# Latent attention with a gated feed-forward: the rope swaps' transfers on ScalarE's queue instead of SyncE's

## What is computed

```
xn = layernorm(x)
q = (xn @ wq) per head: 128 q_nope, 64 q_pe;   kva = xn @ wkv_a: 64 ckv, 64 k_pe
ckv = rmsnorm(ckv) * kv_norm_scale;            k_nope, v = ckv @ wkv_b per head
q_pe, k_pe = rope(q_pe), rope(k_pe)            # [x1*cos - x2*sin, x2*cos + x1*sin]
out = softmax(causal(q k^T / sqrt(192))) v @ wo
g = silu(((silu(xn gate_w^T * gate_s)) * (xn up_w^T * up_s)) down_w^T * down_s)
return x + out * g
```

## Time and profile before

| | |
|---|---|
| time, median of 3 runs (lowest to highest) | 1220.86 us (1214.34 to 1222.77) |
| the profiled execution: its time, its span | 1209.94 us, 1208.1 us |
| TensorE: matmul, weight load | 83%, 71% of the span |
| VectorE, ScalarE, GpSimd | 69%, 60%, 54% |
| granted TensorE clock, mean | 0.93 |

### The profile page before, as it was taken

How to read it: one execution, slowest core, us unless ns; L and a number is a source line. 1 busy time by engine, 2 the same in 40 slices (tenths; PEclk the granted TensorE clock), 3 DMA queues, 4 the chain that set the end, 5 groups by cost and what they waited for, 6 DMA issues and landing times.

```text
span 1208.1 us, 26429 instructions
## 1 busy us (share of the span) xinstructions
PE 1006.8 (83%) x10576; PEld 859.9 (71%) x10576; DVE 828.0 (69%) x1359; ACT 720.4 (60%) x1033; POOL 655.2 (54%) x448
## 2 busy tenths in 40 slices
PE   6665888888888888798888878888798987888998
PEld 5554767777777766677767767677677776777887
DVE  6755766876677777777787668777867687583234
ACT  1336666666667666666666566666766676673222
POOL 3837466745665466655674566465736664531232
PEclk7877998998899999999999899999999899898999
DMA  5038899998999989989999899999989899994001
GB/s 153 18 60 172 153 159 185 189 170 166 176 186 158 180 181 163 177 165 182 176 171 168 167 177 171 169 176 180 183 163 172 171 177 198 164 176 97 1 19 53
DMA packets 600042, 184.92 MB, mean 153 GB/s; under 512 B 574960, under 2 KB 586864, under 8 KB 599920
## 3 DMA queue, kind: packets, MB, share of 16 engines
q1 hardware_dynamic: 595440, 182.57, 81.0%
q10 hardware_dynamic: 4480, 0.66, 0.3%
HBM read 30.09 MB, written 2.10 MB: 27 GB/s over the span
## 4 chain that ended last, share of the span: by engine, by line
PE 29%; DMA 21%; DVE 16%; SPq 14%; POOL 14%; issue 3%; ACT 1%; ACTq 0%; POOLq 0%
DMA pT<-hl 16%; PE s_ps L637 9%; PE s_ps L535 7%; POOL hl L1097 6%; PE slot_ps L535 5%; DVE part_max L937 5%; SPq L478 5%; DMA sinT<-sinT_dram 4%; DVE hl L946 4%; SPq L465 4%; SPq L471 4%; POOL pe L1097 4%; PE o_ps L653 2%; POOL q_swap L1097 2%; PE o_ps L535 1%
## 5 line engine op out<-in xcount | busy, mean ns | idle before, releaser
L807 ACT ACTIVATE prob<-s_ps,neg_max 128x1024 f32<-128x1024 f32 (+7 forms) x384 | 327.6, 864 | 288.8 <-DVE neg_max L940 139.8
L1097 POOL TENSOR_TENSOR hl<-prob,hl 128x1024 f16<-128x1024 f32 x128 | 274.9, 2148 | 262.5 <-ACT hl L743 255.5
L937 DVE TENSOR_REDUCE part_max<-s_ps 128x1 f32<-128x1024 f32 (+7 forms) x256 | 245.2, 987 | 213.7 <-PE s_ps L637 202.8
L653 PE MATMUL o_ps<-v,pT 128*128 128x65 f16 x2176 | 238.2, 197 | 153.6 <-DMA pT<-hl 150.1
L653 PEld LDWEIGHTS o_ps<-v,pT 128*128 128x128 f16 x2176 | 206.9, 98 | 169.3 <-DMA pT<-hl 165.1
L743 ACT ACTIVATE hl<-prob 128x1024 f16<-128x1024 f32 (+7 forms) x384 | 294.9, 804 | 0.0
L946 DVE TENSOR_TENSOR hl<-prob,hl 128x1024 f16<-128x1024 f32 (+7 forms) x256 | 248.9, 1011 | 0.4 <-ACT hl L743 0.4
L654 PE MATMUL o_ps<-v,pT 128*128 128x64 f16 x2176 | 238.2, 198 | 0.0
L655 PE MATMUL o_ps<-v,pT 128*128 128x65 f16 x2176 | 237.1, 195 | 0.0
L655 PEld LDWEIGHTS o_ps<-v,pT 128*128 128x128 f16 x2176 | 209.0, 102 | 0.0
L654 PEld LDWEIGHTS o_ps<-v,pT 128*128 128x128 f16 x2176 | 208.0, 99 | 0.0
(11 more groups left out here) (196 smaller groups left out, 2007.9 us busy)
## 6 DMA issues: line engine op xcount, KB each, us to landing
cosT<-cosT_dram SPq DMA_DIRECT2D x32, 256.0 KB, 3.5
sinT<-sinT_dram SPq DMA_DIRECT2D x32, 256.0 KB, 3.9
q_swap<-q_pe SPq DMA_DIRECT2D x128, 64.0 KB, 2.0
pT<-hl SPq DMA_TRANSPOSE x256, 4.9
wq_sb<-in_L_attn_wq_dram SPq DMA_DIRECT2D x8, 384.0 KB, 4.5
acc<-in_L_attn_x_dram SPq DMA_DIRECT2D x4, 512.0 KB, 6.5
wo_sb<-in_L_attn_wo_dram SPq DMA_DIRECT2D x8, 256.0 KB, 3.3
x_in<-in_L_attn_x_dram SPq DMA_DIRECT2D x1, 2048.0 KB, 8.3
```

Source lines behind the costliest of these rows:

```text
L653: nc.tensor.matmul(whole, pT[:, b, :], v[:, kb, 0:LORA + 1], start=(m != 1 and b == 0), stop=False)
L807: nc.scalar.activation(prob_of(u, m), score_bank(u, m), ACT.Exp, bias=neg_max[:, r:r + 1]).then_inc(exp_done, 1)
L937: nc.vector.tensor_reduce(part_max[:, u % 2, m:m + 1], src, AX.X, ALU.max).then_inc(part_done, 1)
L1097: return lambda: nc.gpsimd.tensor_tensor(dst, a, b, op)
```

## The change

The function `swap` moves from SyncE's program to ScalarE's. ScalarE calls it directly behind the copy into `q_pe`, with the same two waits and the same four transfers; SyncE no longer has them.

```diff
@@ SyncE
-            def swap(g, pair):
-                half = ROPE // 2
-                sp.wait_ge(act_freed, after("act", (f"pe{g}", pair)))
-                n = group_no(g, pair)
-                if n >= 1:
-                    before = GROUP_ORDER[(n - 1) % NG], (n - 1) // NG
-                    sp.wait_ge(pool_done, POOL.after((f"rope{before[0]}.2", before[1])))
-                for i in range(4):
-                    a, b = slice(i * half, (i + 1) * half), slice((i ^ 1) * half, (i ^ 1) * half + half)
-                    sp.dma_start(q_swap[a, :], q_pe[b, :]).then_inc(swapped, 16)
...
-            swap(3, 0)
-            swap(0, 0)
             for u in range(NU):
                 pair, k = divmod(u, PU)
                 turn_first(u)
-                for name in jobs_at(u - 1):
-                    if name[0].startswith("pe"):
-                        swap(int(name[0][2:]), name[1])
                 turn_rest(u)
@@ ScalarE
+            def swap(name, pair):
+                half = ROPE // 2
+                n = group_no(int(name[2:]), pair)
+                act.wait_ge(act_freed, after("act", (name, pair)))
+                if n >= 1:
+                    before = GROUP_ORDER[(n - 1) % NG], (n - 1) // NG
+                    act.wait_ge(pool_done, POOL.after((f"rope{before[0]}.2", before[1])))
+                for i in range(4):
+                    a, b = slice(i * half, (i + 1) * half), slice((i ^ 1) * half, (i ^ 1) * half + half)
+                    act.dma_start(q_swap[a, :], q_pe[b, :]).then_inc(swapped, 16)
...
                     copy(q_pe[:], ps).then_inc(act_freed, 1)
+                    swap(name, pair)
```

## The result

| | before | after |
|---|---|---|
| time, median (lowest to highest) | 1220.86 us, 3 runs (1214.34 to 1222.77) | 1238.66 us, 4 runs (1233.41 to 1249.2) |
| profiled execution: time, span | 1209.94, 1208.1 us | 1239.47, 1237.6 us |
| granted TensorE clock | 0.933 | 0.933 |

The changed kernel is slower: ratio 1.0166, 95% interval 1.0089 to 1.0243, some 18 us. The forecast was 1227, and of its cases "within 1%" had the best chance (0.38). What came is "slower by over 1%" (0.34): above the forecast's own range (1216 to 1237) and inside the wide one (1197 to 1264), which reached that far only because it covers the rivals. The time lies between the forecast (+6) and rival B (+29).

A forecast was written before the change was run, and what follows sets the result against it. It took SyncE's queue, with swaps at 1.5 us each, to be on the path. Per pair -1.2 (unit 6), -1.2 (unit 9), +3.0 (unit 14 with unit 12's gain) made +0.6; together +6 us, 1227, own range 1216 to 1237.

The forecast's parts named there:

- within 1%: Whole kernel: time less than about 12 us from before, no difference that can be told; chance 0.38.
- slower by over 1%: Whole kernel: slower by more than about 12 us, through rivals B and C and a little of the forecast's spread; chance 0.34.
- rival B: ScalarE bounds ten units a pair; delays eat units 6 and 9's gain, unit 14 costs 3.8 us: 1250 us, chance 0.20.
- Units 6, 9 and 12: Second transposes and tables go out earlier once SyncE is rid of the swap: gains 1.2, 1.2 and 0.8 us.
- the late exponentials are covered by SyncE: Units 6 and 9: next unit's exponentials move from 387.43 to 388.8 and 412.76 to 413.4, hidden by SyncE's lateness.
- its cut of unit 6 from 1.9 to 1.2: Unit 6: transpose 1.9 us earlier, but POOL's low half of unit 8 can gain only 0.7; 1.2 taken.
- The hold: ScalarE at each swap: held 2.6 us, four issues at the median 0.584 us each plus some 0.15 for the copy.
- rival C: Swap issues on ScalarE wait for transposes being issued half the time, 32 x 1.4 = 45 us more: 1272 us, chance 0.13.
- Unit 14: ScalarE stands still for rope.2 until 454.2, then issues until 456.7; unit 15's exponentials come late, cost 3.0 us a pair.
- See nothing behind it to take it up: Behind unit 14: nothing later absorbs the 3.0 us delay, so it counts in full.
- +2 for the start: First pair's own swaps: two in the set-up at 0.5 us, those in units 0 and 1 +1.5 us.
- Rival A: SyncE's queue is all that counts; ScalarE's delays vanish under its waits, unit 14 costs 1.1 us: 1207 us, chance 0.27.

The follow-up runs named there:

- e4: Against the changed kernel: no swap transfers and no waits for them, q_swap set to zero once; 1183.14 us, 0.9685 of before.
- e1: Against the changed kernel: only unit 14's swap goes back to SyncE, the others stay on ScalarE; 1219.5 us, 1.0012 of before.
- e5: Against the changed kernel: rope.1 writes into the sine table's buffer, so the swap waits only for rope.1; 1234.58 us, 1.0157 of before.
- e6: Against the changed kernel: the swap goes to the end of ScalarE's unit, behind the high halves; 1236.06 us, 1.0177 of before.
- e9: Against the changed kernel: swaps of units 6, 9 and 12 stay on ScalarE, unit 14's is left out; 1212.74 us, 0.9936 of before.
- e3: Against the kernel before: swaps stay on SyncE, ScalarE only waits for rope.2 behind its copy; 1219.08 us, 0.9998 of before.
- e7: Against the kernel before: swap stays on SyncE but goes behind the second transpose and the tables; 1207.31 us, 0.9896 of before.
- e12: Against the changed kernel: GpSimd issues the swap last in its unit, behind the steps of rope; 1199.0 us, 0.9825 of before.
- e11: Against the changed kernel: swap on GpSimd, last in its unit, the same kernel as e12, run earlier; median 1206.89 us, 0.989 of before.
- e10: Against the changed kernel: unit 14's swap stays on ScalarE, those of units 6, 9 and 12 are left out; 1214.25 us, 0.9976 of before.
- e8: Against the kernel before: GpSimd issues the swap, ahead of rope.0, instead of SyncE; 1220.21 us, 1.0034 of before.

## Why the prediction was right and wrong

**What bounds the kernel: right.** SyncE's queue was on the path for about 1.5 us a swap, 48 in all by the chain; taking the swaps away gave 34 us (e4). In unit 6, 9, 12 and 14 the second transpose had started 2.5, 2.0, 1.4 and 2.5 us behind the last low half (means of pairs 2 to 7, from the timelines of SyncE and VectorE); in after it is 0.03 in all four.

**Units 6, 9 and 12: the failed step.** The text took gains of 1.2, 1.2 and 0.8, 3.2 a pair, of which the first stretch shows 0.5, within the noise. That relief was there to be had: e4 has 3.5. The step that failed is how late the hold makes VectorE's low halves. The text has "389.8 instead of 388.73" in unit 6, "about 414.4" instead of 414.06 in unit 9, and for unit 12 "the hold hardly moves them": 1.1, 0.3 and 0. Against the first transpose of the unit the last low half ends 1.9, 1.4 and 1.4 us later in after than in before (means of six pairs), 4.6 in all in place of 1.4. So of the 5.9 us by which SyncE had been late only 1.2 are won: the second transpose less the first went from 5.63 to 5.06 us in unit 6, from 5.26 to 4.62 in unit 9, from 6.26 to 6.25 in unit 12. Without swaps it is 3.48, 2.92 and 4.77, so the change won a fifth of what relief alone gives.

Unit 12 shows how. The "other work of VectorE" ahead of the low halves takes its input from two copies of ScalarE (`QA_hi`, `QB_hi`), which stand behind the swap as well. VectorE in unit 12 of after, third pair:

```profile
447.64 0.69 DVE L889 TENSOR_TENSOR QA_lo<-slot_ps,QA_hi 64x512 fp32r<-64x512 f32 x1 [1.17 <-ACT QB_hi L726]
...
448.96 1.41 DVE L942 TENSOR_TENSOR hl<-prob,hl 128x512 f16<-128x512 f32 x2
```

The other part of that step, that the late exponentials are covered by SyncE, held on average at the next first transpose. The first transposes of units 7, 10 and 13 still start 0.1 us behind the item ahead of them in SyncE's queue, and GpSimd's low half has been ready for 0.9, 0.4 and 1.0 us (3.4, 2.6 and 2.3 in before). Little of the cover is left. The five units without a swap give back 0.7 of the 1.1 us that the three won, which the text had at nothing apart from its cut of unit 6 from 1.9 to 1.2; in e4 they give back 2.3 of 5.7, with no hold at all.

Reading a single place misled too: in the third pair's unit 6 the second transpose was 6.65 us behind the copy's end before (385.02 to 391.67) and 5.05 after, 1.6 of the 1.9 foretold, where the mean over pairs, against the first transpose, shows 0.6. The copy of before:

```profile
384.42 0.60 ACT L743 ACTIVATE q_pe<-slot_ps 128x512 f32<-128x512 f32 x1 [0.24 <-PE slot_ps L535]
```

**The hold.** Taken as 2.6 us: 2.44 for the four issues, and 0.15 for the copy, for which no row was given. The rows of after have 0.03 from the copy's end to the first issue and 0.10 behind the last. From the copy's end to the next instruction of ScalarE it is 3.03, 3.43 and 3.24 us in units 6, 9 and 12 (mean over the seven pairs), though the median issue is 0.614. Half of the excess was in the kernel before already: four issues took 2.44 us at the median there, but 2.76 in the mean of these three units, and a term that is added up 32 times wants the mean. On ScalarE the mean is 3.09. The move itself makes 0.3 us a swap, which is a part of rival C, instead of its 1.4.

Here the Trainium skill can be weighed (Perfetto Trace Analysis, "DMA Instruction — HWDGE (DVE, Sync)": one descriptor block, locked for one sequencer at a time). The section names the sequencers of VectorE and SyncE; the prediction took the rule over to ScalarE's and SyncE's. SyncE of after, unit 12 of the third pair, and ScalarE at the same time:

```profile
442.08 3.41 SPq L459 DMA_TRANSPOSE pT<-hl  x1
```

```profile
442.45 3.86 ACTq L738 DMA_DIRECT2D q_swap<-q_pe  x4
```

The four issues took 0.52, 0.61, 1.84 and 0.80 us. Two of them pass beside the transpose's 3.41 at the usual length, and the third ends at 445.48, when the transpose's issue does (445.49). With the lock held for the whole of it, the first would have ended there. Over all of after, 79 of the 128 issues overlap with a transpose's: their median is 0.614 as that of the others (0.613), their mean 0.751 against 0.632, and of the 12 over 1.1 us ten are among them, five of which end within 0.3 us of the transpose's end. The same difference of the means shows in e1, e5, e6 and e9 (0.07 to 0.18 us). Long issues come without any transpose of another queue as well: in before 7 of the 128 on SyncE were over 1.1 us. So the figures fit something shared, as the rule says, but it would hold an issue up only now and then and cost 0.1 us on average, no full wait. C's mechanism is at most a small part of the hold; the forecast had it at nothing.

**Unit 14: right in the mechanism.** Foretold were a standstill of about 4.2 us behind the copy, 2.5 of issuing, exponentials 6.3 and the first transpose of unit 15 2.3 us late, and a cost of 3.0 a pair with unit 12's gain in it, 3.8 without. Seen were 4.2 and 2.5 (the rows of ScalarE in unit 14), unit 14 longer by 3.0 (8.4 to 11.4) and the second stretch longer by 3.6: the gross price, since unit 12 gave nothing ahead of it. The second transpose, the text's lower bound for the cost, carries none of it (e6). And the wait was priced together with the issues: alone it would have cost about 0.3 (e3). "See nothing behind it to take it up" holds for what exceeds four microseconds; the first four are taken up beside SyncE's own chain.

**The sum.** With the measured terms: -0.5 in the first stretch and +3.6 in the second are +3.1 a pair, 22 over seven, and +2 for the start as foretold makes 24; the medians differ by 18, the profiled executions by 29.5. The forecast was short by the 2.7 us that units 6, 9 and 12 failed to give, not by unit 14. Rival B is near as a sum ("eat the gain there", with 0.5 left in place of none), but its way is another than the one seen: it has the delays of units 6 and 9 reach the following units, and they are paid at the second transposes of 6, 9 and 12 themselves. Its test, ScalarE's slack under 1.3 us, looks at the wait ahead of the exponentials, where little was lost. Rival A falls: it needed ScalarE's delays to vanish under its waits and unit 14 to cost 1.1 us, and e9 has 3.2 us a pair for the first, the stretch 3.6 for the second. That the wide range held the time owes more to its width than to the terms: the gain of three units was four fifths wrong and the loss of one was right.

**The price of an issue against its transfer.** In the earlier trace rows one issue is 0.584 us, four with gaps 2.44, and by the page of before a transfer lands 2.0 us behind its issue at the median. The Trainium skill (DMA: Bandwidth & Descriptors, "Issuing engines are not separate DMA queues") says that starting transfers on several engines saves only the initiating time on a sequencer, "which is usually small relative to the DMA itself". For four transfers of 64 KB it is not small. The same transfers from another place of the same queue (e7) or from another queue (e12, after) made the time 0.9896, 0.9825 and 1.0166 of before, although no byte was moved otherwise.

## What to carry to other kernels

A DMA issue costs its queue as much as a small computation costs an engine: 0.584 us here, where ScalarE's copy of 128x512 takes 0.60. So before moving one, list all that stands behind it on the new queue, and also what other engines make from that (in unit 12 VectorE's work ahead of the low halves). What the old queue wins is its lateness less the new delay of whatever it waits for next; take both as means over many places, not from one. A transfer that waits for another engine's step can go on that engine's own queue, behind the step and ahead of an idle time of its own (e12, 0.9825; e11, 0.989), and often it is enough to let the urgent transfers of the same queue pass first (e7, 0.9896); these runs don't tell the two apart. A wait on a busy engine can be free up to the slack that something parallel gives it, and the same wait with 2.5 us of issues behind it is then paid in full: test the two apart.

## What the runs showed of the hardware

- The swap's transfers land later from the other queues: median 2.0 us from SyncE in the kernel before, 3.4 from ScalarE in after (4.3 in e9, with those of units 6, 9 and 12 alone, and 2.0 in e10, with those of unit 14), 3.9 and 4.8 from GpSimd in e12 and e8. From SyncE behind the tables (e7) it is 2.7, so the queue alone doesn't set it. On SyncE they are issued between two transposes or behind them, on the others often beside one; whether that is the cause was not tried. GpSimd waited only 2.7 us for them in all of after.
- GpSimd's issues are the steadiest: 0.496 to 0.740 us, median 0.498, against up to 1.7 on SyncE and 2.7 on ScalarE.
- The time of one kernel follows the granted clock. In 72 executions of the kernel before, timed beside the experiments, the mean granted clock lay between 0.920 and 0.945 and the time between 1229.9 and 1208.3 us; a straight line through them falls 6.7 us for each 0.01, and they scatter about it by 3.7 us (standard deviation). Against that line, at their own clocks, after is 22 us above, e4 25 below, e9 2 below, e10 level, e7 7 and e12 11 below. So the order of these kernels and the sum of the halves (-25 + 23 + 25 = +23) don't hang on the clock. Whether a faster kernel is granted more of it, or has it by chance, stays open.
